# A graph kernel's counting stage: h kept in x's buffer, bn_stats, four PSUM banks, 52 fills, and high one-hots with the eight edges innermost

## What is computed

```python
h = relu(layernorm(x))                       # mean and variance over 128, eps 1e-5
# layer 0: attention over edges
hW = (h @ W).reshape(N, 4, 32)
alpha = leaky_relu(s_src[row] + s_dst[col])  # s_src, s_dst: hW against two vectors per head
# softmax of alpha over the edges of one source row, then
x = x + segment_sum(alpha_n * hW[col], col) + bias
# layer 1: an MLP over edges
h = relu(layernorm(x))
msg = relu(concat([h[row], h[col], edge_attr]) @ W1 + b1) @ W2 + b2
x = x + segment_sum(msg, row)                # row = src, col = dst
```

## Time and profile before

| | us |
|---|---|
| median of 3 executions | 6986.6 (6968.1 to 6987.1) |
| the profiled execution, its own time | 6995.8 |
| its span in the profile | 6994.0 |
| busy in the span: PE, PEld | 4638.7, 3778.8 |
| busy: DVE, ACT, POOL | 3616.0, 3051.2, 3267.5 |

### The profile page before, as it was taken

The page is one execution under the profiler, slowest core; times in us unless marked ns, Lnnn a source line. Parts: engine busy times, 40 slices in busy tenths (PEclk is TensorE's granted clock), DMA queues, the critical chain, the costliest instruction groups (busy, mean ns, idle before and its releaser), DMA issues. The chain is left out here.

```text
span 6994.0 us, 98927 instructions
## 1 busy us (share of the span) xinstructions
PE 4638.7 (66%) x22798; PEld 3778.8 (54%) x22799; DVE 3616.0 (52%) x8020; ACT 3051.2 (44%) x4592; POOL 3267.5 (47%) x3490
## 2 busy tenths in 40 slices
PE   5766666666666666630699866666666666666667
PEld 4655545555555455520599745555555555555556
DVE  8733333333333333327999845555555555555555
ACT  4433333333333333311577644444444444444444
POOL 2355555555555555560000045555555555555553
PEclk9977776777777777765799988888888888888888
DMA  8743333333333333389100254444444444444446
GB/s 299 267 109 102 103 99 104 101 104 103 104 104 101 99 105 102 104 102 49 45 0 0 73 137 103 106 104 107 102 108 106 109 104 107 103 110 105 107 103 104
DMA packets 1214122, 735.03 MB, mean 105 GB/s; under 512 B 929899, under 2 KB 1031461, under 8 KB 1213965
## 3 DMA queue, kind: packets, MB, share of 16 engines
q1 hardware_dynamic: 864716, 348.63, 23.6%
q0 software_dynamic: 131616, 276.04, 14.0%
q10 hardware_dynamic: 217760, 110.04, 5.5%
HBM read 562.85 MB, written 165.09 MB: 104 GB/s over the span
## 5 line engine op out<-in xcount | busy, mean ns | idle before, releaser
L1053 POOL DMA_INDIRECT g_q<-q_d,g_aux x1664 | 1579.6, 949 | 2195.3 <-DMA pw<-g_q 900.5
L571 POOL DMA_INDIRECT rec_d<-rec,place x1568 | 1535.5, 979 | 1225.1 <-DVE place L634 758.1
L1366 PE MATMUL g_ap<-g_hid,g_oh 128*128 128x256 f32 x3328 | 1094.6, 461 | 854.5 <-DVE agg L1158 688.6
L1366 PEld LDWEIGHTS g_ap<-g_hid,g_oh 128*128 128x128 f32 x3328 | 736.0, 232 | 1054.1 <-issue 797.2
L684 PE MATMUL lk<-tab_sd,low 128*128 128x196 f32 x3136 | 1141.8, 446 | 190.8 <-issue 190.4
L1272 ACT ACTIVATE g_hid<-g_q 128x512 f32<-128x512 f32 x832 | 524.0, 630 | 1513.1 <-DVE g_q L1144 1325.3
L1158 DVE TENSOR_TENSOR agg<-agg,g_ap 128x256 f32 x1664 | 690.7, 415 | 863.0 <-remote 744.0
L1355 PE MATMUL g_hp<-pw,g_mix 128*128 x3328 | 1026.7, 438 | 62.4 <-issue 40.4
L620 DVE TENSOR_REDUCE rank<-equal 128x4 f32<-128x512 bf16 x392 | 268.3, 685 | 1546.8 <-ACT equal L548 1197.9
L548 ACT ACTIVATE equal<-rk,minus_two 128x512 bf16<-128x512 f32 x392 | 268.0, 684 | 1706.4 <-remote 1098.4
L1355 PEld LDWEIGHTS g_hp<-pw,g_mix 128*128 128x128 f32 x3328 | 738.5, 225 | 243.5 <-issue 112.6
(11 more groups left out here) (229 smaller groups left out, 5120.4 us busy)
## 6 DMA issues: line engine op xcount, KB each, us to landing
low_row<-rows_d SPq DMA_DIRECT2D x392, 256.0 KB
g_ea<-rec_d SPq DMA_DIRECT2D x208, 256.0 KB
rec<-in_ea ACTq DMA_DIRECT2D x196, 256.0 KB
rec_d<-pad ACTq DMA_DIRECT2D x49, 936.0 KB, 3.8
hx_row<-rows_d SPq DMA_DIRECT2D x392, 98.0 KB
g_lrow<-low_row_d SPq DMA_DIRECT2D x208, 128.0 KB
g_q<-q_d,g_aux POOLq DMA_INDIRECT x1664
rec_d<-rec,place POOLq DMA_INDIRECT x1568
```

The costliest lines, as they stand in the source:

```text
L571: pool.indirect_dma_start(rec_d, bass.IndirectOffsetOnAxis(ap=place[0:n, at, j:j + 1], axis=0), rec[0:n, at, j, :], None).then_inc(s_sc[at ...
L1053: pool.indirect_dma_start(qg[:, par, j, :], None, q_d, bass.IndirectOffsetOnAxis(ap=aux[:, par, j, F_IDX - F_LOW:REC - F_LOW].bitcast(I32) ...
L1366: mm = pe.matmul(ap[u % 2][:, k * HID:(k + 1) * HID], oh[:, par, 2 * u + k, :], hid[:, u, k, :], start=True, stop=True)
```

## The change

It has six parts.

1. Statistics by bn_stats (L355 of the changed kernel) for each of 49 blocks, each giving mean and spread of two halves, and four small operations that join them; eps goes into the root's bias. cent and ACT's square of all x are gone. h is relu(x / std - mean / std), from xs itself with scale and bias.
2. The product's result is written to the block's own place in xs, which is no longer needed, and stored from there; hrow and the wait for its store are gone.
3. Four PSUM banks for the four groups of a step: the matmuls of group g wait for the copy of group g - 4.
4. FILL is 32: 52 fills of 1152 KB, 3 by SP ahead and 49 in the steps. The loads of dst_i and of flat_i's second half go from SP's queue to ACT's.
5. The index field of the pad records, 0 before, is p + 192 c for partition p and place c of a fill.
6. oh_high has its axes turned, 49 digits by eight edges innermost, as oh_low has. VectorE makes it from iota_g, and TensorE's moving operand has a step of eight elements.

```diff
-FILL = 26
+FILL = 32
+ROW_STEP = (NODES_P - P) // FILL
...
-                oh_high = freed_b[:, FOUR * GE:FOUR * (GE + G * NB)].rearrange("p (k j a) -> p k j a", k=FOUR, j=G)
+                oh_high = freed_b[:, FOUR * GE:FOUR * (GE + G * NB)].rearrange("p (k a j) -> p k a j", k=FOUR, j=G)
...
-                hist = [pb(f"hist{k}", ctx) for k in range(2)]
+                hist = [pb(f"hist{k}", ctx) for k in range(FOUR)]
...
                     sp.dma_start(xs[:, :, :], x.rearrange("(b p) d -> p b d", p=P)).then_inc(s_in, 16)
-                    sp.dma_start(flat_i[:, 1, :], dst_t.rearrange("(p c) -> p c", p=P)).then_inc(s_flatd, 16)
-                    sp.dma_start(dst_i[:, :, :], dst_v).then_inc(s_dstl, 16)
-                    sp.wait_ge(s_pad, 3)
+                    sp.wait_ge(s_pad, 4)
...
                         sp.dma_start(h_d.rearrange("(b p) d -> b p d", p=P)[bass.ds(it, 1), :, :].rearrange("o p d -> (o p) d"),
-                                     hrow[:, :]).then_inc(s_hs, 16)
+                                     xs[:, bass.ds(it, 1), :].rearrange("p o d -> p (o d)")).then_inc(s_hs, 16)
...
+                    pool.iota(pad[:, :, F_IDX].bitcast(I32), [[ROW_STEP, FILL]], base=0, channel_multiplier=1).then_inc(s_pad, 1)
...
-                    v.wait_ge(s_in, 16)
-                    link(v.tensor_reduce(st[:, 0, :], xs[:, :, :], X, ALU.add))
-                    link(v.tensor_scalar(st[:, 1, :], st[:, 0, :], 1.0 / D, None, ALU.mult))
-                    v.tensor_tensor(cent[:, :, :], xs[:, :, :], col(st[:, 1, :], P, NB, D), ALU.subtract).then_inc(s_cent, 1)
...
-                    v.wait_ge(s_sq, 1)
-                    link(v.tensor_reduce(st[:, 2, :], xs[:, :, :], X, ALU.add))
-                    v.tensor_scalar(st[:, 3, :], st[:, 2, :], 1.0 / D, EPS, ALU.mult, ALU.add).then_inc(s_var, 1)
+                    v.wait_ge(s_in, 16)
+                    for b in range(NB):
+                        v.bn_stats(bn[:, b, :], xs[:, b, :]).then_inc(s_bn, 1)
+                    v.wait_ge(s_bn, NB)
+                    v.tensor_tensor(pair[:, :, :], bn[:, :, 1:3], bn[:, :, 4:6], ALU.add)
...
-                        v.tensor_tensor(oh_high[:, k, :, :], col(tile(high_src), P, G, NB), row(iota_b[:, 0:NB], P, G, NB),
-                                        ALU.is_equal).then_inc(s_oh, 1)
+                        v.tensor_tensor(oh_high[:, k, :, :], row(tile(high_src), P, NB, G), iota_g[:, 0:NB, :], ALU.is_equal).then_inc(s_oh, 1)
...
-                        if not begin:
-                            pe.wait_ge(s_pre, g - 1)
+                        if not first(g, FOUR):
+                            pe.wait_ge(s_pre, g - (FOUR - 1))
                         for j in range(G):
-                            mm = pe.matmul(hist[par][:, j * NB:G * NB], oh_low[:, k, :, j],
-                                           row(oh_high[:, k, j, :], P, G - j, NB), start=(j == 0), stop=(j == G - 1),
+                            mm = pe.matmul(hist[k][:, j * NB:G * NB], oh_low[:, k, :, j],
+                                           row(oh_high[:, k, :, j], P, G - j, NB), start=(j == 0), stop=(j == G - 1),
...
+                    act.dma_start(dst_i[:, :, :], dst_v).then_inc(s_dstl, 16)
+                    act.dma_start(flat_i[:, 1, :], dst_t.rearrange("(p c) -> p c", p=P)).then_inc(s_flatd, 16)
...
-                    act.wait_ge(s_cent, 1)
-                    act.activation(xs[:, :, :], cent[:, :, :], ACT.Square).then_inc(s_sq, 1)
...
-                        if not first(it):
-                            act.wait_ge(s_hs, it * 16)
-                        act.activation(hrow[:, :], mp[:, 0:D], ACT.Copy)
+                        act.activation(xs[:, bass.ds(it, 1), :].rearrange("p o d -> p (o d)"), mp[:, 0:D], ACT.Copy)
```

More of the change, by code:

```diff
@@ L193, in build @@
                 hT = sb("hT", [P, P], F32, ctx)
-                hrow = sb("hrow", [P, D], F32, ctx)
                 wx = sb("wx", [P, D + 2 * HEADS], F32, ctx)
@@ L370, in _ @@
                     v.wait_ge(s_std, 1)
-                    v.reciprocal(st[:, 1, :], st[:, 0, :]).then_inc(s_rstd, 1)
+                    link(v.reciprocal(st[:, 1, :], st[:, 0, :]))
+                    v.scalar_tensor_tensor(out=st[:, 2, :], in0=pair[:, :, 0], scalar=-0.5, in1=st[:, 1, :],
+                                           op0=ALU.mult, op1=ALU.mult).then_inc(s_rstd, 1)
                     for k in range(1, FOUR):
@@ L395, in step @@
                         pe.transpose(tp[:, 0:P], hb[:, :], ident[:, :]).then_inc(s_t, 1)
-                        count(it * FOUR, 0, first(it))
-                        count(it * FOUR + 1, 1, first(it))
+                        count(it * FOUR, 0)
+                        count(it * FOUR + 1, 1)
                         pe.wait_ge(s_hT, it + 1)
@@ L441, in moved @@
                             act.wait_ge(s_tot, g - 2)
-                        act.activation(pre[:, k, :], hist[k % 2][:, 0:G * NB], ACT.Copy).then_inc(s_pre, 1)
+                        act.activation(pre[:, k, :], hist[k][:, 0:G * NB], ACT.Copy).then_inc(s_pre, 1)
                     def normed(it):
-                        act.activation(hb[:, :], cent[:, bass.ds(it, 1), :].rearrange("p o d -> p (o d)"), ACT.Relu,
-                                       scale=st[:, 1, bass.ds(it, 1)]).then_inc(s_h, 1)
+                        act.activation(hb[:, :], xs[:, bass.ds(it, 1), :].rearrange("p o d -> p (o d)"), ACT.Relu,
+                                       bias=st[:, 2, bass.ds(it, 1)], scale=st[:, 1, bass.ds(it, 1)]).then_inc(s_h, 1)
                     def step(it, last=False):
```

23 lines of the change are left out of this document (15 added, 8 removed).

## The result

| | before | after |
|---|---|---|
| median, same chip | 6983.6 (6968.1 to 6987.1, 4 executions) | 7356.1 (7346.1 to 7370.8, 4 executions) |
| ratio, 95% interval | 1 | 1.0525 (1.0506 to 1.0544) |
| profiled execution, span | 6994.0 | 7344.3 |
| first transpose | 51.26 | 37.57 |
| end of the counting stage (copy into deg) | 334.0 | 702.4 |

The kernel became 5.25% slower; 0.7% had been forecast, with a range that ended at 7090. All of it is in the counting stage: it ends 368.4 us later, the rest is 18.1 us shorter, together the 350.3 us between the spans.

A forecast was written before the change was run, and what follows sets the result against it. Counting loop bound by hrow's copy-store-landing ring before, by TensorE after: 49 x 6.96 plus holes 1 and 8, drain 6, is 356.0 against 282.8, +73.2; start -15.0, pads -8: +50.2, 7037 on the median. Range 6968 to 7090.

The forecast's parts named there:

- the pace of 0.88 ns a column: Counting matmuls on TensorE: the stepped moving operand comes at the weights' pace, 0.88 ns a column; chance 0.66.
- a group 1.62, a step 6.96: Counting loop: eight matmuls of a group take 1.62 us, four groups plus 0.48 make a step of 6.96 us.
- the nearest rows are the weights of the same matmuls: Counting matmuls: stepped weight loads, 0.113 us each, stand in for the stepped moving operand, which no row shows.
- Start: Before the counting loop: digits first, then 49 bn_stats; first transpose at 36.3 instead of 51.26, 15.0 us earlier.
- rival 4: VectorE's high one-hots don't get cheaper: 4.6 us a step hide under 6.96, forecast stays; no chance given.
- it would make 0.23: VectorE in the counting loop: at the low one-hots' rate the high ones' 392 elements would take 0.23 us.
- Rival 1: Counting loop: the stepped moving operand is free, step 4.5 us, 67.8 us faster, 6919 in all; chance 0.19.
- DMA is next: Counting loop with matmuls unchanged: once hrow's wait goes, DMA bounds a step at 4.5 us, 3.02 + 1.49.
- the first hole: Early in the counting loop, ACT's wait for a prefix store: 12.11 us before, 1 forecast, ends 0 and 3.
- Pads: Last 52 tiles' gathers: spread filler indices instead of one row of q save 8 us, ends 0 and 17.
- the other end: Counting matmuls: the moving operand's step costs nothing at all, a group stays at 0.835 us.
- the shared fetch: Counting matmuls: weights and moving operand share one fetch, group 1.87 us, step 7.96, 7086 in all; chance 0.06.

The follow-up runs named there:

- e2: The kernel before with only the layout of the high one-hots changed, so the moving operand is stepped: 7380.2 us, ratio 1.0557 to the kernel before.
- m1: Microbenchmark of matmuls alone, nothing of the reference computed, with ten forms of operands: a 392-column matmul took 867 ns at step 8, 329 contiguous in the sixty.
- e1: The changed kernel with its high one-hots laid out as before, moving operand contiguous: 6955.8 us, ratio 0.9951 to the kernel before.
- e6: e1 with eight buffers for the prefix rows instead of four, and a looser wait for POOL's sum: 6932.3 us, ratio 0.9925 to the kernel before.
- e3: The changed kernel with the axes of oh_low turned so that TensorE's weights are contiguous, moving operand still stepped: 7332.3 us in a single execution.

## Why the prediction was wrong, point by point

**The mechanism held.** TensorE without idle time, ACT and VectorE waiting for hist, no wait ahead of the copy of h, DMA share under 0.65, first transpose between 35 and 40: all as written, and e2 shows that the stepped moving operand alone does it.

**The term that failed** is the pace of 0.88 ns a column, and with it "a group 1.62, a step 6.96". It measured 1.78 in the kernel: a group of 3.18, a step of 13.46. 49 x (13.46 - 6.96) = 318.5 is the whole miss in the stage: 310 between its end at 392 and at 702; the forecast also had 9 us of holes, which the slow loop doesn't have.

The step that led there was this: "the nearest rows are the weights of the same matmuls", 16 loads in 1.83 us, 0.113 each. Two things were wrong with it. The spacing of those loads wasn't their own pace: a group's 1764 columns at 0.42 ns are 0.74 us of its 0.835, so the loads came as the matmuls let them, and by themselves a stepped load follows the last after 0.064 us. And the weights' side has another price for a line than the moving side. The first mistake even made the number larger, and hid how far apart the two sides are. What the loads' 144 ns against 98 showed rightly was only that a step of 16 bytes isn't free.

**The rule.** On the Trainium skill, "SBUF — State Buffer", section "Door 1: The DMA port swizzle (why `[64,N]` ≈ `[32,N]`)", the text sided with the sentence that full bandwidth wants two hits in each 16-byte line, against the one that eight bf16 can be stepped over for free. The runs bear the 16-byte line out, and at a step of eight the second sentence is off by a factor of four. But the first was used only as a direction. At the full clock two hits are not enough: step 2 (four hits) runs at 0.44 ns, step 3 (2.67) at 0.66, step 4 (two) at 0.88. Two are enough at the low level only, where step 4 and contiguous data took 525 and 531 ns.

**The clock.** The text took the transpose and the product at their times at the upper clock level, 0.48 us a step. In the kernel after, L404 takes 482 ns instead of 331 and L398 411. By these durations it is the lower level, though the column PEclk reads 1.00 in that stretch, as it does for the first ten of m1 beside 531 ns. Two stretches of m1, with contiguous data and with a step of eight:

```profile
54.30:64.10 9.80, 9.80 (x61) 5.75 (x59) 0.00 (x0) 0.00 (x0) 1.00 0.01 2
...
226.30:250.90 24.60, 24.60 (x36) 4.37 (x35) 0.00 (x0) 0.00 (x0) 0.50 0.00 0
```

With contiguous data the granted clock is 1.00, at a step of eight it comes down to 0.50 with the engine busy throughout. The matmuls of the step can't confirm that column, being as long at 1.00; L404's 482 ns in the kernel do. The low level costs the counting matmuls nothing, since theirs is the pace of the lines; the two others take 0.76 us a step instead of 0.48.

**Start.** 36.3 forecast, 37.57 measured. The bn_stats came at 23.91 and took 9.57 us (9.8 forecast); they had to wait 1.12 us for x:

```profile
23.91 9.57 DVE L355 BATCH_NORM_STATS2 bn<-xs 128x6 f32<-128x128 f32 x49 [1.12 <-DMA xs<-in_x]
```

**VectorE's high one-hots** got cheaper, 0.35 to 0.44 us for 0.55 to 0.67, so rival 4 falls; "it would make 0.23" was too low. All of it lies under TensorE.

**The other parts' value.** Rival 1 had 4.5 us a step, bound by DMA's bytes, and a stage end near 274. e1 shows 5.05 and 305.6, and a hole of 11.8 where 10.5 stood. The step that failed is "DMA is next": a DMA share of 0.86 and a landing time grown from some 2.3 to 3.2 us keep a ring of four buffers from reaching it. Only with eight (e6) does the stage end at 284.7, and then VectorE, at 4.63 us a step, is ahead of DMA or level with it. The 4.5 itself was a little high (0.86 of 5.05 is 4.3), and the first hole, for which the forecast had 1 us, is gone in e1.

**Pads.** 8 forecast with ends 0 and 17; the profiled execution has 18 behind the stage, but the kernels with equal code there differ by as much (6635.7 for e3, 6651.9 for e6). The 2.0 us a tile of the ten microseconds was a short sample, as the text feared: over the hundred microseconds above it is 2.9 before and 2.8 after.

**Range and chances.** The range was sized by rivals near the weights' rate, since "the other end" for the unknown was the cheap one, no cost at all. For the dear side the text had only the shared fetch, 1.87 us a group. An operand that no row showed should have had an upper bound from a row of its own kind, or none: the moving operand's price went from 0.44 at a step of 2 to 1.76 at a step of 8.

## What to carry to other kernels

A layout that makes VectorE's write cheap can move its cost to the matmul that reads it: count how many different 16-byte lines the moving operand touches, and give each about 1.76 ns. Contiguous bf16 (0.42 ns a column) and a step of two (0.44) are all but free of it at the full clock; every layout tried that leaves fewer than four columns in a line is not, and here that cost more than VectorE could save. And before the spacing of instructions is read as their pace, look whether they are the ones that wait.

When a wait for a store is taken away, look for the next buffer whose store lands behind the same large transfer: doubling it gave 20.9 us here, and e6, without the layout, is faster than both kernels, at 0.9925.

## What the runs showed of the hardware that was not expected

- Moving operand, bf16: 1.76 ns for each 16-byte line touched, the same at both clock levels (867 ns in both), with 64 partitions as with 128, and flat from a step of 8 to one of 32 (1.67 to 1.79).
- Weights: 0.027 us between contiguous loads of 128 columns, 0.037 at a step of 4, 0.064 at a step of 8 or 16, which is 0.50 ns a column.
- TensorE at a step of 8 came down to a granted clock of 0.50 (m1, from 218 us on) while it was busy all the time.
- Seven loads issued among the prefix stores made holes of 8.7 and 8.3 us, fourteen one of 10.3: stores issued late by the loads' issue time (4.4 us for seven, 9.6 for fourteen), and, for the seven, landings of 11.7 instead of 6.6 us.
